# A fused vision tower: moving attention's product with V behind the next scores, and the FFN weights' quantising forward

## The chip, the cores and the metric

One core of one Trainium2 chip. The time is the device time of one execution in microseconds. The kernel before takes 271.56 us, the median of 3 runs (271.5 to 272.1).

## The reference

A two-layer tower on 16 images of 36 tokens (T = 576) and 192 channels: patch embedding, attention with 12 heads of 64, a feed-forward layer (FFN) with quantised weights and activations, then a second layer (test-time-training attention and 8 experts) that the change does not touch. Cut to the part concerned:

```
h = patches @ W_proj.T + b_proj
xn = layernorm(layernorm(h)) * gamma + beta
q, k, v = split(xn @ w_qkv)                       # 12 heads of 64
out = softmax(q @ k.T / 8) @ v                    # within an image: 36 keys
h = h + out @ w_out + b_out

def weight_quant(w):                              # FFN weights w_in, w_out
    scale = 1.0 / max(mean(abs(w)), 1e-5)
    return clip(round(w * scale), -1, 1) / scale
h = h + bitlinear(gated(bitlinear(layernorm(h), w_in)), w_out)
... second layer
```

## The kernel before

Every engine has one hand-written instruction stream; engines meet through semaphores. In a stream, an instruction that waits holds up everything behind it.

**Precision.** Nearly every fp32 operand x is split into two f16 parts, a high one (ACT copies x to f16) and a low one (DVE forms x minus the high part). A product is three f16 products, so most results leave PSUM twice: first by ACT (high), then by DVE (low), which also frees the bank.

**PSUM.** The 8 banks go round in the order of `plan(...)`, which is the order of PE's work. PE claims a bank when its last user has been read (`claim`); `wait_full` waits for a bank to be filled, `wait_evac` for it to be read, `frees` marks that.

**Order of the stages.** Embedding, normalisation, V for five tiles of 128 tokens (L552), two pairs of small products for the sums of the FFN weights' magnitudes (L558, L559), keys and queries for the first 8 images (L568), then the attention loop with `PAIRS + 4` = 12 turns s = 0 to 11, then the rest of the output projection and the FFN.

**The attention loop** is a software pipeline over pairs of images, PAIRS = 8. In turn s:

- PE: the product with V of pair s-4 (L609, `values`), the transposes of the probabilities of pair s-3, high and low part into two banks (L623), in turns 0 to 2 four banks of keys and queries of the second 8 images (`keys_queries`, L568), the scores of pair s+1 (L597, `scores`), in turns 8 to 10 a tile of the output projection (L582).
- DVE: the sum of the exponentials of pair s-1 (L1064) and its reciprocal (L1067), the maximum of the scores of pair s (L1071) and the subtraction (L1074), the low half of the probabilities of pair s-2 (L1081), in turns 0 to 2 the low halves of two heads' keys (L1018) and queries (L1025), the low half of the product with V of pair s-4 (L1090), and the work laid between: the clipping of the FFN weights, w_out (`stage2`, L1093, L1094) in turn 3 and w_in (`stage13`, a view of `stage_a`, L1096, L1098) in turns 4 and 5; the low half of the attention's w_out (L1101) in turn 7, which the output projection awaits (`wo_lo`); preparation of layer 2's weights (`state_weights`) in turn 9; residuals (L1054) from turn 9.
- GpSimd (POOL): the probabilities times the reciprocals (L1797).
- ACT: the high half of the probabilities of pair s-2 (L1545), the high half of the product with V of pair s-4 (L1549), the copy of the transposed high part of pair s-3 (L1556), exp of pair s (L1559), the copy of the transposed low part (L1563), in turns 0 to 2 high halves of keys and queries (L1529, L1534), the attention's w_out to f16 (L1569) in turn 5, the quantised FFN w_out (L1575) in turn 6; behind the loop the quantised w_in (L1577) and a table load.

The means of the FFN weights are finished on DVE (L1007 to L1012) before the first keys are read. The raw attention w_out (`woraw`) is loaded by SP behind the 32 loads of V; it lies in the arena that GpSimd's expert weights use later, so these wait for `wo_lo` (`expert_high`).

Of the kernel before, what the change touches and what calls it, by code (L numbers as in the profile page):

```python
# [23 lines left out]
FH = 512  # L24
# [20 lines left out]
NROW = _at  # L45

# [5 lines left out]
def tower(nc, d, out):  # L52

    ctx = ExitStack()
    with ctx:
# [241 lines left out]
        plan("wmean")  # L297
# [4 lines left out]
        for s in range(PAIRS + 4):  # L302
            if 0 <= s - 4:
                plan("PV", s - 4)
# [3 lines left out]
            if s < 3:  # L308
                for hp in (2 * s, 2 * s + 1):
                    plan("k", hp, 1)  # L310
                    plan("q", hp, 1)
            if s + 1 < PAIRS:
                plan("S", s + 1)
            if PAIRS <= s < PAIRS + 3:
                plan("wo", s - PAIRS)
# [107 lines left out]
        def expert_high(pool, e):  # L423
# [3 lines left out]
            if e == 4:  # L427
                wait_full(pool, "S", PAIRS - 1)
                pool.wait_ge(wo_lo, 1)
# [21 lines left out]
        def _(sp):  # L451
# [34 lines left out]
            wait_full(sp, "q", HP - 1, 1)  # L486
# [27 lines left out]
        def _(pe):  # L514
# [40 lines left out]
            bk = claim(pe, "wmean")  # L555
            pe.wait_ge(wq_part, 2)
            pe.wait_ge(zeroed, 1)
            mm(bk[:, 0:1], ones[0:HF, :].broadcast_to([HF, 128]), wsum[0:HF, 0:1], start=True, stop=True)  # L558
            ins = mm(bk[:, 1:2], ones[:, :].broadcast_to([128, 128]), wsum[:, 1:2], start=True, stop=True)  # L559
            fills(ins, "wmean")  # L560
# [53 lines left out]
            for s in range(PAIRS + 4):  # L614
                if 0 <= s - 4:
                    values(s - 4)
# [8 lines left out]
                if s < 3:  # L625
                    for hp in (2 * s, 2 * s + 1):
                        keys_queries(hp, 1)
                if s + 1 < PAIRS:
                    scores(s + 1)
                if PAIRS <= s < PAIRS + 3:  # L630
# [311 lines left out]
        def _(dve):  # L942
# [48 lines left out]
            dve.wait_ge(loaded("w_in"), 16)  # L991
            dve.wait_ge(loaded("w_out2"), 16)
            v.tensor_reduce(wsum[0:HF, 0:1], stage13[:, :, :], AX.XY, ALU.add, apply_absolute_value=True).then_inc(wq_part, 1)
            v.tensor_reduce(wsum[:, 1:2], stage2[:, :, :], AX.XY, ALU.add, apply_absolute_value=True).then_inc(wq_part, 1)
# [9 lines left out]


            bk = wait_full(dve, "wmean")
            st_.do(v.tensor_scalar(mw[:, 0:1], bk[:, 0:1], 1.0 / (2 * FH * D), 1e-5, ALU.mult, ALU.max))  # L1007
# [949 lines left out]
```

## Time and profile before

| | us |
|---|---|
| median of 3 runs | 271.56 |
| the profiled execution | 269.44 |
| its span, first to last instruction | 267.6 |
| PE busy in the span | 223.1 |
| DVE busy | 191.0 |
| ACT busy | 154.6 |
| GpSimd busy | 115.9 |

The busy times are averages over stages with different limits. The attention loop runs from about 51 to 102 us. The rows further below come from its timeline: each line gives start, length, engine, source line, operation, output and inputs with their shapes, the number of instructions merged, and in brackets how long the engine had been idle and what it waited for ("issue" where the profile shows no releaser). Instructions on DVE and ACT overlap a little: the next starts up to 0.1 us before the end of the last.

### The profile page before, as it was taken

What the parts mean: (1) busy time and instruction counts of PE and PEld (TensorE: products, weight loads), DVE (VectorE), ACT (ScalarE), POOL (GpSimd) and SP (SyncE); (2) the same over time, 40 slices, a digit from 0 to 9 for tenths busy, and PEclk for the clock granted to TensorE, in tenths of its full rate; (3) what the DMA queues carried; (4) which work ended last, traced back from release to release, by engine and by line L of the source; (5) the groups of instructions that cost most, each with busy time, mean ns of one, the idle gap of its engine ahead of it and who ended that gap; (6) DMA issues with size and microseconds to landing.
All of it is one profiled execution on the core that took longest, in us unless ns stands there. A gap on an engine that the chain in (4) does not pass through costs nothing.

```text
span 267.6 us, 6168 instructions
## 1 busy us (share of the span) xinstructions
PE 223.1 (83%) x2338; PEld 174.5 (65%) x2338; DVE 191.0 (71%) x520; ACT 154.6 (58%) x296; POOL 115.9 (43%) x139
## 2 busy tenths in 40 slices
PE   1964999797396897797989999899899695999992
PEld 1741467586396896344458596786648595899982
DVE  1749979767999577869958869649786352655575
ACT  4639467355679755378579758557461265455610
POOL 9112495011122696476390002502602887867710
PEclk9996599999779599999999999999999999999997
DMA  6999352332540049993009001994290599883362
GB/s 213 336 257 216 82 224 65 71 69 68 164 146 4 2 67 205 212 210 67 4 0 108 2 0 10 119 138 62 13 173 12 100 147 160 144 124 31 35 154 66
DMA packets 24786, 28.66 MB, mean 107 GB/s; under 512 B 11544, under 2 KB 19793, under 8 KB 24533
## 3 DMA queue, kind: packets, MB, share of 16 engines
q0 software_dynamic: 6624, 13.66, 34.0%
q1 hardware_dynamic: 18133, 14.60, 19.2%
q8 instruction: 19, 0.31, 0.5%
q14 instruction: 10, 0.08, 0.1%
HBM read 34.98 MB, written 4.81 MB: 149 GB/s over the span
## 4 chain that ended last, share of the span: by engine, by line
PE 43%; DVE 26%; ACT 9%; issue 8%; POOL 1%; DMA 1%; another core or an unknown queue 1%; DVEq 0%; ACTq 0%; POOLq 0%
PE bank L885 7%; PE bank L896 5%; PE bank L552 5%; PE bank L637 4%; PE bank L568 3%; PE bank L727 2%; PE bank L609 2%; DVE arena_k L1018 2%; PE bank L597 2%; PE bank L704 2%; PE bank L582 2%; DVE st L949 2%; PE bank L834 1%; DMA arena<-x_scratch,arena 1%; PE bank L745 1%
## 5 line engine op out<-in xcount | busy, mean ns | idle before, releaser
L637 PE MATMUL bank<-tri,idh 128*128 128x512 f16 x148 | 38.5, 380 | 0.0
L1797 POOL TENSOR_TENSOR arena<-arena,ri 128x432 f32<-128x432 f32 x8 | 7.5, 942 | 39.3 <-DVE ri L1067 39.3
L1773 POOL TENSOR_TENSOR rs<-arg,mhalf 128x1 f32<-128x1 f32 (+1 forms) x20 | 11.9, 596 | 23.1 <-DVE arg L953 21.6
L1875 POOL DMA_INDIRECT arena<-x_scratch,arena x14 | 14.1, 1006 | 16.7 <-DVE arena L1431 12.7
L1866 POOL DMA_INDIRECT y_sum<-arena x12 | 18.2, 1515 | 6.3 <-issue 2.9
L1383 DVE TENSOR_TENSOR arena<-bank,arena 128x360 f32<-128x360 f32 x16 | 8.4, 532 | 16.8 <-PE bank L885 8.5
L637 PEld LDWEIGHTS bank<-tri,idh 128*128 128x128 f16 x148 | 13.7, 98 | 9.7
L568 PE MATMUL bank<-arena,arena_k 96*128 96x288 f16 (+2 forms) x144 | 18.3, 286 | 0.0
L525 PE MATMUL bank<-arena_v,arena 128*128 128x192 f16 (+1 forms) x90 | 11.6, 295 | 5.9 <-DVE arena_v L967 5.9
L568 PEld LDWEIGHTS bank<-arena,arena_k 96*128 96x128 f16 x144 | 13.8, 98 | 3.5
L885 PE MATMUL bank<-arena,arena_v 128*128 128x180 f16 x160 | 13.4, 240 | 2.9 <-DVE arena L1372 2.6
L597 PE MATMUL bank<-arena_k,arena 128*64 128x72 f16 x288 | 11.3, 210 | 5.0 <-DVE arena L1025 5.0
L444 POOL DMA_DIRECT2D arena_v<-in_w x4 | 3.2, 806 | 27.2 <-ACT arena_v L439 27.2
L885 PEld LDWEIGHTS bank<-arena,arena_v 128*128 128x128 f16 x160 | 12.4, 97 | 4.0 <-DVE arena L1372 3.3
L597 PEld LDWEIGHTS bank<-arena_k,arena 128*64 128x64 f16 x288 | 10.4, 122 | 6.4 <-issue 6.3
L552 PE MATMUL bank<-arena_k,arena 96*128 96x384 f16 (+1 forms) x60 | 13.3, 394 | 1.5 <-DVE arena_k L980 1.5
L525 PEld LDWEIGHTS bank<-arena_v,arena 128*128 128x128 f16 (+1 forms) x90 | 9.0, 119 | 8.3 <-DVE arena_v L967 6.2
L1018 DVE TENSOR_TENSOR arena_k<-bank,arena_k 64x288 f16<-64x288 f32 x24 | 10.9, 454 | 4.5 <-ACT arena_k L1529 3.9
L1784 POOL MEMSET arena_v<- 72x12288 f32 x1 | 10.3, 10338 | 7.0 <-DVE arena_k L990 7.0
L1724 ACT ACTIVATE arena<-bank 128x360 f32<-128x360 f32 x16 | 7.3, 470 | 10.5 <-PE bank L885 9.4
L885 PE MATMUL bank<-arena,arena_k 128*128 128x180 f16 x160 | 13.1, 240 | 0.0
L609 PE MATMUL bank<-arena,arena_v 72*128 72x36 f16 x288 | 9.0, 183 | 4.5 <-issue 4.5
(286 smaller groups left out, 634.2 us busy)
## 6 DMA issues: line engine op xcount, KB each, us to landing
arena_k<-in_w POOLq DMA_DIRECT2D x8, 512.0 KB, 6.4
arena_v<-in_w POOLq DMA_DIRECT2D x8, 512.0 KB, 10.2
arena_v<-in_xT SPq DMA_DIRECT2D x6, 288.0 KB, 3.7
arena_v<-in_wqkv SPq DMA_DIRECT2D x3, 576.0 KB, 10.0
arena_v<-v_scratch SPq DMA_DIRECT2D x32, 54.0 KB
v_scratch<-arena SPq DMA_DIRECT2D x4, 384.0 KB, 2.6
arena_k<-in_w POOLq DMA_DIRECT2D x8, 192.0 KB, 7.2
arena_v<-in_w POOLq DMA_DIRECT2D x8, 192.0 KB, 11.2
```

The source lines that it names most:

```text
L525: ins = mm(at_bank("embed", i)[0:r, 0:D], xpT[:, a_, k, 128 * i:128 * i + r], wp16[:, w_, k, :], start=k == 0 and n == 0, stop=k == KC - 1 ...
L552: ins = mm(bk[0:r, 0:384], x16[:, a_, j, 128 * i:128 * i + r], wqkv[:, w_, j, 1536 + 384 * c:1536 + 384 * c + 384], start=n + j == 0, stop ...
L568: ins = mm(bk[:, 0:c1 - c0], wqkv[:, w_, j, o + 128 * hp:o + 128 * hp + 128], x16[:, a_, j, c0:c1], start=m + j == 0, stop=m == 2 and j == 1)
L597: ins = mm(bk[64 * x:64 * x + 64, 72 * hp:72 * hp + 72], qT[:, a_, hp, NP * b:NP * b + 64], Kbd[:, w_, hp, b, :], start=n == 0, stop=n == 2)
L609: ins = mm(bk[:, 72 * hp + NP * x:72 * hp + NP * x + NP], Vbd[:, 2 * p + x, hp].rearrange("p y c x -> p (y c) x")[:, :, w_], PT[:, p % 2, ...
L637: mm(bank[IDLE][:, :], idh[:, :], tri[:, 0:1].broadcast_to([128, 512]), start=True, stop=True)
L885: ins = mm(bk[:, CAP * m:CAP * m + CAP], w[:, wx, j, f:f + 128], z[:, zx, :], start=n == 0, stop=n == 4)
L896: ins = mm(bk[0:SH, D * s:D * s + D], actp2[e % 2][:, ax, m, SH * s:SH * s + SH], w2p[e][:, wx, m, :], start=n == 0, stop=n == 11)
L1018: ins = v.tensor_tensor(Kbd[o, 1, hp, 8 * n:8 * n + 8, NP * x:NP * x + NP], bk[o, 0:288].rearrange("p (b k) -> p b k", k=NP), Kbd[o, 0, hp ...
L1773: g.tensor_tensor(rs[0:r, o + i:o + i + 1], arg[0:r, o + i:o + i + 1], half_[0:r, 0:1], ALU.pow).then_inc(sem_out, 1)
L1866: nc.gpsimd.indirect_dma_start(y_sum[k][:, :], bass.IndirectOffsetOnAxis(ap=sum_at[:, k, e:e + 1], axis=0), ys[:, e, D * k:D * k + D], Non ...
L1875: nc.gpsimd.indirect_dma_start(zr[:, e - 1, XW * k:XW * k + XW], None, x_scr[:, :], bass.IndirectOffsetOnAxis(ap=tok_at[:, k, e:e + 1], ax ...
```

## The change

On PE the product with V moves to the end of its turn, behind the transposes and the next scores. Its two read-outs move as well: on ACT behind exp and the copy of the low transposed part, and on both engines a turn later for the first pairs (pair s-5 in turns 5 to 7, pairs 3 and 4 in turn 8, then pair s-4). The sums of the FFN weights' magnitudes are taken by ACT (Abs with an accumulated sum) between the first keys and the loop, not by DVE before V is read; the products that spread them move from in front of the keys into turn 0, and the means into DVE's turn 0. The clipping moves from turns 3 to 5 to turns 1 and 2, the quantising copies from turn 6 and from behind the loop to turns 2 and 3. `woraw` lies in another arena, and two waits go (SP's before its load, GpSimd's for `wo_lo`).

```diff
+def read_out(s):
+    if s < PAIRS:
+        return range(max(s - 5, 0), max(s - 4, 0))
+    return range(PAIRS - 5 if s == PAIRS else s - 4, s - 3)
...
+        wide = arena[:, KC * T + HP * D:KC * T + HP * D + 2048]
-        woraw = arenaK[:, K_W:K_W + HP * D].rearrange("p (k n) -> p k n", k=HP)
+        woraw = arena[:, KC * T:KC * T + HP * D].rearrange("p (k n) -> p k n", k=HP)
...
-                pool.wait_ge(wo_lo, 1)
...
-            wait_full(sp, "q", HP - 1, 1)
...   # PE; the order of plan() follows it
-            bk = claim(pe, "wmean")   # and its four products
+            def weight_sums():        # the same
             scores(0)
             for s in range(PAIRS + 4):
-                if 0 <= s - 4:
-                    values(s - 4)
                 p = s - 3             # transposes
                 if s < 3:
-                    for hp in (2 * s, 2 * s + 1):
-                        keys_queries(hp, 1)
+                    keys_queries(2 * s, 1)
+                    if s == 0:
+                        weight_sums()
+                    keys_queries(2 * s + 1, 1)
                 if s + 1 < PAIRS:
                     scores(s + 1)
+                if 0 <= s - 4:
+                    values(s - 4)
...   # DVE
-            v.tensor_reduce(wsum[0:HF, 0:1], stage13[:, :, :], AX.XY, ALU.add, apply_absolute_value=True).then_inc(wq_part, 1)
-            v.tensor_reduce(wsum[:, 1:2], stage2[:, :, :], AX.XY, ALU.add, apply_absolute_value=True).then_inc(wq_part, 1)
...   # in the loop, behind the low half of the probabilities
+                if s == 1:
+                    st_.then(v.tensor_scalar(stage2[:], stage2[:], sw[:, 1:2], 1.0, ALU.mult, ALU.min))
+                    v.tensor_scalar(stage2[:], stage2[:], -1.0, MAGIC, ALU.max, ALU.add).then_inc(wq_sum, 1)
+                if s == 2:
+                    st_.settle()
+                    v.tensor_scalar(stage13[:], stage13[:], -1.0, MAGIC, ALU.max, ALU.add).then_inc(wq_sum, 1)
                 if s < 3:
-                    for hp in (2 * s, 2 * s + 1):
-                        kq_low(hp, 1)
-                p = s - 4
-                if 0 <= p:
+                    kq_low(2 * s, 1)
+                if s == 0:
+                    weight_means()
+                if s == 1:
+                    st_.do(v.tensor_scalar(stage13[:], stage13[:], sw[0:HF, 0:1], 1.0, ALU.mult, ALU.min))
+                if s < 3:
+                    kq_low(2 * s + 1, 1)
+                for p in read_out(s):
                     bk = wait_full(dve, "PV", p)
                     dve.wait_ge(ao_hi, p + 1)   # and the subtraction into aoT
-                if s == 3: ...  if s == 4: ...  if s == 5: ...   # the same four passes
...   # ACT, before the loop
+            act.wait_ge(loaded("w_in"), 16)
+            act.wait_ge(loaded("w_out2"), 16)
+            act.wait_ge(v_stored, 16 * NT)
+            for w, n in ((stage_a[0:HF, :], 0), (stage2[:, :, :].rearrange("p m n -> p (m n)"), 1)):
+                r, m = w.shape
+                st_.do(a(wide[0:r, 0:m], w, ACT.Abs, accum_out=wsum[0:r, n:n + 1]))
+                st_.settle()
+            act.sem_inc(wq_part, 2)
...   # ACT, in the loop: behind the high half of the probabilities
-                p = s - 4
-                if 0 <= p:
-                    bk = wait_full(act, "PV", p)
-                    a(aoT[:, 0, :, 72 * p:72 * p + 72], ...).then_inc(ao_hi, 1)
...   # behind exp and the copy of the low transposed part
+                for p in read_out(s):
+                    bk = wait_full(act, "PV", p)
+                    a(aoT[:, 0, :, 72 * p:72 * p + 72], ...).then_inc(ao_hi, 1)
                 if s < 3: ...                   # high halves of keys and queries
+                if s == 2:
+                    act.wait_ge(wq_sum, 1)
+                    a(w2q[:], stage2[:], ACT.Identity, bias=nmagic[:, 0:1]).then_inc(wq_done, 1)
+                if s == 3:
+                    act.wait_ge(wq_sum, 2)
+                    a(wiq[:], stage13[:], ACT.Identity, bias=nmagic[0:HF, 0:1]).then_inc(wq_done, 1)
-                if s == 6: ...                  # w2q
-            act.wait_ge(wq_sum, 2)              # wiq, behind the loop
```

## Rows read from the trace of the kernel before

**Rows 1.** The page, granted clock: tenths of full speed, 40 equal slices.
```profile
PEclk9996599999779599999999999999999999999997
```

**Rows 2.** Timeline, DVE: start, length, engine, line, tiles, count [idle <-releaser].
```profile
60.85 0.92 DVE L1018 TENSOR_TENSOR arena_k<-bank,arena_k 64x288 f16<-64x288 f32 x2 [1.41 <-ACT arena_k L1529]
...
66.81 0.92 DVE L1018 TENSOR_TENSOR arena_k<-bank,arena_k 64x288 f16<-64x288 f32 x2 [0.90 <-ACT arena_k L1529]
```

**Rows 3.** Timeline, DVE, turns 3 to 7: sums (L1064), clipping, scores.
```profile
69.40 0.59 DVE L1064 TENSOR_REDUCE sm<-arena 128x12 f32<-128x432 f32 x1
...
72.92 0.60 DVE L1064 TENSOR_REDUCE sm<-arena 128x12 f32<-128x432 f32 x1
...
75.23 2.01 PE L597 MATMUL bank<-arena_k,arena 128*64 128x72 f16 x36
...
75.83 1.27 DVE L1096 TENSOR_SCALAR stage_a<-stage_a,sw 96x2048 f32<-96x2048 f32 x1
...
77.14 0.60 DVE L1064 TENSOR_REDUCE sm<-arena 128x12 f32<-128x432 f32 x1
...
81.19 0.59 DVE L1064 TENSOR_REDUCE sm<-arena 128x12 f32<-128x432 f32 x1
...
84.09 0.59 DVE L1064 TENSOR_REDUCE sm<-arena 128x12 f32<-128x432 f32 x1
...
88.27 0.59 DVE L1064 TENSOR_REDUCE sm<-arena 128x12 f32<-128x432 f32 x1
```

**Rows 4.** Timeline, turns 5 to 7: ACT and DVE.
```profile
82.46 0.81 ACT L1556 ACTIVATE arena<-bank 72x768 f16<-72x768 f16 x1
...
82.54 0.61 DVE L1074 TENSOR_TENSOR arena<-bank,mx 128x432 f32<-128x432 f32 x1
...
83.18 0.56 ACT L1559 ACTIVATE arena<-arena 128x432 f32<-128x432 f32 x1
...
83.65 0.79 ACT L1563 ACTIVATE arena<-bank 72x768 f16<-72x768 f16 x1
...
84.34 0.92 ACT L1575 ACTIVATE w2q<-stage,nmagic 128x768 f16<-128x768 f32 x1
...
87.00 1.34 DVE L1101 TENSOR_TENSOR arena<-arena_k,arena 128x1152 f16<-128x1152 f32 x1
```

**Rows 5.** Timeline, tail of the attention stage: PE, ACT, DVE.
```profile
88.10 1.24 PE L609 MATMUL bank<-arena,arena_v 72*128 72x36 f16 x36 [1.82 <-issue]
...
90.44 3.09 PE L582 MATMUL bank<-arena 128*128 128x192 f16 x18
...
94.37 0.84 PE L623 MATMUL bank<-idh,arena 128*72 128x128 f16 x12
...
94.56 0.53 ACT L1549 ACTIVATE arena<-bank 128x432 f16<-128x432 f32 x1 [1.76 <-PE bank L609]
...
95.05 1.65 PE L582 MATMUL bank<-arena 128*128 128x192 f16 x18
...
95.19 0.61 DVE L1090 TENSOR_TENSOR arena<-bank,arena 128x432 f16<-128x432 f32 x1 [1.19 <-ACT arena L1549]
```

**Rows 6.** Timeline, before the first scores: means of the weights, ACT's wait.
```profile
39.16 0.38 PE L558 MATMUL bank<-wsum,ones 96*128 96x1 f32 x2
...
40.46 0.13 DVE L1007 TENSOR_SCALAR mw<-bank 128x1 f32<-128x1 f32 x1
...
40.84 0.56 DVE L1012 TENSOR_SCALAR mwd<-mw 128x2 f32<-128x2 f32 x1
...
53.51 0.56 ACT L1559 ACTIVATE arena<-arena 128x432 f32<-128x432 f32 x1 [3.96 <-DVE arena L1074]
```

**Rows 7.** Timeline, ACT behind the attention loop.
```profile
101.49 1.99 ACT L1577 ACTIVATE wiq<-stage_a,nmagic 96x2048 f16<-96x2048 f32 x1
...
103.49 1.28 ACT L1497 ACT_TABLE_LOAD   x1
...
108.56 0.47 ACT L1584 ACTIVATE arena<-bank,nmagic 96x256 f16<-96x256 f32 x1 [3.57 <-PE bank L648]
```

More of the change, by code:

```diff
@@ L311, in tower @@
                     plan("q", hp, 1)
+                    if hp == 0:
+                        plan("wmean")
             if s + 1 < PAIRS:
                 plan("S", s + 1)
+            if 0 <= s - 4:
+                plan("PV", s - 4)
             if PAIRS <= s < PAIRS + 3:
@@ L554, in _ @@
                     fills(ins, "v", i, c)
-            bk = claim(pe, "wmean")
[L556 to L560, printed above, removed]
+            def weight_sums():
+                bk = claim(pe, "wmean")
+                pe.wait_ge(wq_part, 2)
+                pe.wait_ge(zeroed, 1)
+                mm(bk[:, 0:1], ones[0:HF, :].broadcast_to([HF, 128]), wsum[0:HF, 0:1], start=True, stop=True)
+                ins = mm(bk[:, 1:2], ones[:, :].broadcast_to([128, 128]), wsum[:, 1:2], start=True, stop=True)
+                fills(ins, "wmean")
             def keys_queries(hp, n):
@@ L1058, in _, with weight_means @@
             dve.wait_ge(hbias, 1)
+            def weight_means():
+                bk = wait_full(dve, "wmean")
+                st_.do(v.tensor_scalar(mw[:, 0:1], bk[:, 0:1], 1.0 / (2 * FH * D), 1e-5, ALU.mult, ALU.max))
+                frees(v.tensor_scalar(mw[:, 1:2], bk[:, 1:2], 1.0 / (FH * D), 1e-5, ALU.mult, ALU.max), "wmean")
+                st_.settle()
+                wait_evac(dve, "wmean")
+                st_.do(v.reciprocal(sw[:], mw[:]))
+                st_.then(v.tensor_scalar(mwd[:], mw[:], 1.0 / 127.0, None, ALU.mult))
             for s in range(PAIRS + 4):
@@ L1091, in _ @@
                                           ALU.subtract), "PV", p)
-                if s == 3:
-                    st_.then(v.tensor_scalar(stage2[:], stage2[:], sw[:, 1:2], 1.0, ALU.mult, ALU.min))
-                    v.tensor_scalar(stage2[:], stage2[:], -1.0, MAGIC, ALU.max, ALU.add).then_inc(wq_sum, 1)
-                if s == 4:
-                    st_.then(v.tensor_scalar(stage13[:], stage13[:], sw[0:HF, 0:1], 1.0, ALU.mult, ALU.min))
-                if s == 5:
-                    v.tensor_scalar(stage13[:], stage13[:], -1.0, MAGIC, ALU.max, ALU.add).then_inc(wq_sum, 1)
                 if s == PAIRS - 1:
@@ L1563, in _ @@
                     frees(a(PT[:, p % 2, 1, :], bk[0:72, :].bitcast(F16)[:, 0:768], ACT.Copy), "PT", p, 1)
+                for p in read_out(s):
+                    bk = wait_full(act, "PV", p)
+                    a(aoT[:, 0, :, 72 * p:72 * p + 72], bk[:, 0:432].rearrange("p (h q) -> p h q", h=HP),
+                      ACT.Copy).then_inc(ao_hi, 1)
                 if s < 3:
@@ L1572, in _ @@
                     a(wa16[:, 0], wa[:, :, :], ACT.Copy).then_inc(tw_hi, 1)
-                if s == 6:
-                    act.wait_ge(wq_sum, 1)
-                    a(w2q[:], stage2[:], ACT.Identity, bias=nmagic[:, 0:1]).then_inc(wq_done, 1)
-            act.wait_ge(wq_sum, 2)
-            a(wiq[:], stage13[:], ACT.Identity, bias=nmagic[0:HF, 0:1]).then_inc(wq_done, 1)
             table(ACT.Silu)
```

16 lines of the change are left out of this document (2 added, 14 removed).

## The prediction, made before the result

> **What bounds the kernel now.** Start with the granted clock on the page, one digit for each 6.7 us [rows 1]. In the attention stage (50 to 102 us) the digits 7, 7 (67 to 80 us) and 5 (87 to 94 us) say that TensorE falls to its lower level (1.2 GHz) there twice, so PE is not what is full: the stage is a chain over four engines, and the question is which wait closes its turn. The timeline answers that. A turn runs from one start of L1064 (DVE's sum of the exponentials) to the next.
>
> - Turns 0 to 2, 5.96 us each, are DVE's: maximum, subtraction, then a hole while ACT does exp and the first copy of keys (1.41 us in turn 1, 0.90 us in turn 2 [rows 2]), then the low halves of keys and queries without a gap.
> - Turns 3, 4 and 5 take 72.92 - 69.40 = 3.52, 77.14 - 72.92 = 4.22 and 81.19 - 77.14 = 4.05 us [rows 3]. DVE has no hole in them: the clipping of the FFN weights lies there (L1096 takes 1.27 us).
> - Turn 6 has no clipping and takes 2.90 us (81.19 to 84.09), turn 7 has woT's low half (L1101, 1.34 us) and takes 4.18 us [rows 3, 4].
> - After that PE leads. The product with V at 88.10 had waited 1.82 us, and the first output projection, at the slow clock, takes 3.09 us where a later one takes 1.65 us [rows 5].
>
> The end hangs on DVE's in-order queue. L1090 of pair 5 starts at 95.19 [rows 5]. Behind it come the state weights and residual(0), whose bank output projection 2 needs, then PV(7), its two read-outs, residual(2) and the FFN. The change touches nothing in that row of work, so I carry one number through: the start of L1090 for pair 5.
>
> **The change part by part.** Everything is counted in the profiled execution (269.44 us, span 267.6 us). The runs of before have the median 271.56 us, 2.12 us above it; I add my difference to the median.
>
> *Sums of the weights off DVE, onto ACT.* DVE loses two reductions before 34 us. They bring nothing: the keys start by PE's order, behind V, and DVE waits for ACT's first copy of keys, not ACT for DVE. PE loses the small products between V and K. The first pair takes 0.38 us and all of K waits behind it [rows 6], so **-0.38 us**; at most twice that, and 0 if DVE's read-out of V decides there. ACT's two Abs passes come where ACT waits 3.96 us for the first scores [rows 6]. By L1577, 2048 columns in 1.99 us [rows 7], 2048 and 768 columns cost 1.99 + 0.75 us; that leaves 1.22 us of the hole for reading out the two sums and the two settles, of which no row shows the cost. The hole opens and closes with the keys and moves as a whole; I take **0**, and each us beyond 1.22 would be a us of the stage.
>
> *Means on DVE, moved to turn 0* between two low halves. From L1007's start at 40.46 to L1012's end at 41.40 it is 0.94 us [rows 6]. It used to lie before the first keys were there; now it lies behind turn 0's hole, where DVE has no other, so **+0.94 us** (0 to 0.94).
>
> *Clipping moved.* stage2's two passes (turn 1) fall into the hole of 1.41 us and cost nothing. stage13's first pass stands between the low halves of turn 1, behind the hole: **+1.27 us**. Its second pass (turn 2, taken as 1.27 us like the first, same tile) meets a hole of 0.90 us: **+0.37 us**. Turn 2 thus ends 2.20 us later. The lower bound for all of this is 0, if ACT's copies rather than DVE set these turns.
>
> *Turn 3* loses its clipping and has no read-out. DVE then waits for exp: L1074 starts 1.35 us into a turn, exp starts 0.64 us later and takes 0.56 us, plus 0.05 us [rows 3, 4]: 2.60 instead of 3.52 us, **-0.92 us**.
>
> *Turn 4.* The quantising of w_in (L1577, 1.99 us [rows 7]) moves from behind the loop, where ACT later sat idle for 3.57 us waiting for PE [rows 7] (so nothing is gained there), to ACT's turn 3. Behind it in ACT's queue are the high half of P(2), the copy of PT(1) and exp(4); DVE's next sum waits for that. Start to start on ACT [rows 4, 5, 7]: from exp(3) 0.47 to the copy of PT(0), 0.69 to w_in, 1.90 to the high half of P(2) (1.99 less an overlap of 0.09), 0.45 from that (as many columns as the 0.53 us read-out, less the overlap) to the copy of PT(1), 0.72 (0.81 less the same) to exp(4). That is 4.23 us from exp to exp, and the sums behind them stand as far apart: **0** against turn 4's 4.22. w2q (0.92 us) moves into turn 2, where ACT waits for DVE's subtraction anyway: 0.
>
> *Turns 5 to 7: the read-out.* This is the step that I think decides. ACT's high half of PV used to stand before exp in ACT's turn, so that it was done when DVE came to L1090. Now it stands behind exp and behind the copy of PT's low part, while DVE's L1090 still stands before DVE's next sums, and the next exp waits for DVE's subtraction. That closes a loop in every turn. From L1074's start: exp +0.64, copy +0.47, read-out on ACT +0.69 (the next start behind the copy), its 0.53 us, +0.10 to L1090, +0.51 to the sum (0.61 less the overlap), +1.35 to the next L1074 (81.19 to 82.54) [rows 4, 5]: **4.29 us**. DVE stands idle for about 1.2 of it. Turn 5 was 4.05 (**+0.24**), turn 6 was 2.90 (**+1.39**), and turn 7, with L1101's 1.27 us (87.00 to 88.27), comes to 5.56 instead of 4.18 (**+1.38**). Bounds: 2.90 us a turn if DVE never waits for that read-out, and 4.7 us a turn if PE runs at the lower clock (1.24 for PV, 2.01 for the scores, twice the quick 0.84 for the transposes [rows 3, 5], less some 0.2 of overlap).
>
> Sum up to the sum of pair 7: -0.38 + 0.94 + 1.27 + 0.37 - 0.92 + 0 + 0.24 + 1.39 + 1.38 = **+4.29 us**, so 92.56 instead of 88.27.
>
> *The tail gives part back.* PE's new order no longer holds the transposes behind the product with V, so PT(5) and PV(4) are done while woT's low half is awaited. The first output projection starts 0.1 us after 92.56. Then it takes 1.65 us quick or 3.09 us slow [rows 5]; PE has worked for some 2 us before it, so I take the middle, 2.4. Then PT(6) 0.84, PV(5) 1.24, +0.05, ACT's 0.53, +0.10: L1090 for pair 5 at 92.56 + 5.26 = 97.82, against 95.19. The tail costs 5.26 instead of 6.92 us: **-1.66 us** (-0.97 to -2.41 by the two clocks). Turn 8 reads out pairs 3 and 4 together, which ACT and DVE have done before PV(5) is ready.
>
> *The rest* costs nothing: woT lands in another place but is issued at the same point of SP's queue, after the loads of V; GpSimd's wait for wo_lo goes, but behind its last product with the reciprocals it has rows of its own to make first, and the weight's low half behind those waits for ACT's turn 8. From residual(0) on everything moves as a whole.
>
> Result: +4.29 - 1.66 = **+2.63 us**: 272.1 us in a profile like this one, and as a median **274.2 us**.
>
> **Two rules beside the rows.** Of the clock, the rows show that the digit falls to 5 around the product that had waited 1.82 us [rows 1, 5]. The Trainium skill, page "TensorE: Matmul & The Clock Gate", section "Why this matters for your kernels", says that idle gaps between bursts of products send the clock back to its lower level. A loop in which PE waits for DVE in every turn leaves such gaps. By that rule the first output projection would be slow throughout, and the sum +3.3 us; by the middle of the two rows it is the +2.63 above. Of tables, the row shows that one load takes 1.28 us [rows 7]. The skill's page "ScalarE: Activation LUTs", section "Table sets: the hidden batching unit", says that abs is in every set; by that the Abs passes bring no load, and by the opposite the third rival below holds.
>
> **The rivals.**
> 1. *Faster: the loop through the read-out doesn't bind.* PE's waits for ACT's copies go (1.82 us once [rows 5]), and turns 5 to 7 run at DVE's 2.90 us. That takes (4.29 - 2.90) x 3 = 4.17 us off: 2.63 - 4.17 = -1.54 us, **270.0 us**. For it: PE's order is better by itself. Against: the order on ACT and DVE, as above. It decides once DVE's wait before L1090 is under 0.6 us a turn.
> 2. *PE becomes the bound at the slow clock.* Turns 5 to 7 take 4.7 us (+1.2) and the first output projection 3.09 us (+0.7): +4.5, **276.1 us**. It decides from the point where PE's three pieces of a turn pass 4.29 us. For it: the clock digits after a pause. Against: the digit is 9 from 80 to 87 us [rows 1], through turn 6.
> 3. *The Abs passes reload tables.* Two loads of 1.28 us [rows 7] on top of 2.74 us, and half of the 1.22 us for the reads, overrun the 3.96 us by 1.95: 2.63 + 1.95, **276.1 us**.
> 4. *No difference.* The three insertions of turns 0 to 2 fall into slack, because ACT's copies set those turns (-2.58 us, so +0.05): **271.6 us**. Against: DVE goes from one low half to the next without a gap.
>
> **How the numbers follow.** My forecast 0.50 (its own range 273.4 to 275.2), rival 1 0.13, rival 2 0.20, rival 3 0.05, rival 4 0.12. A change under 0.2% (0.54 us) can't be told from none here. Faster is rival 1, 0.13; the same is rival 4, 0.12; slower is the rest, 0.75. The range 271.0 to 276.2 leaves out rival 1 and the upper edge of rivals 2 and 3, under 2 in 10.
>
> **What would show it.** In the profile after: the first L568 product some 0.4 us earlier; no table load between 40 and 60 us; the hole before turn 1's low halves filled, that turn near 7.2 us; turn 3 near 2.6 us; in turns 5 to 7 DVE idle for some 1.2 us each before the low read-out of PV, released by ACT's high one, with 4.3 us from sum to sum; the first output projection released by woT's low half near 92.6 us; the low read-out of pair 5 near 98 us; all after that unchanged in length. The forecast is wrong if that idle time is missing, or if the stretch from the first scores to the last low read-out is not longer than before.

## The result and the profile after

Over 4 runs the changed kernel takes 275.79 us (274.44 to 277.68) beside 271.83 us before: 1.0144 times as long, 95% interval 1.0092 to 1.0195, or +3.9 us (the 271.83 is the three runs of before given above and one more). Timed again among the experiments (12 runs beside 29 of before) it stands at 1.0088 (1.0050 to 1.0125), +2.4 us. All ratios here leave out the executions that took over 1.5% longer than the fastest of the same kernel. The change makes the kernel slower: neither interval reaches 1. In the two profiled executions the last read-out of attention (DVE, pair 7) starts at 104.88 us instead of 101.69: +3.19 us.

The page after, its span and the granted clock:

```profile
span 272.6 us, 6168 instructions
...
PEclk9996699998588589999999999999999999999996
```

From 61 to 102 us, the turns and the tail, the clock's digits are 8, 5, 8, 8, 5, 8; before, the low ones were 7, 7 and 5 [rows 1]. The tail's fall to the lower clock (the second 5, 89 to 95 us) is still there.

The timeline of the changed kernel, DVE's sums of the exponentials (L1069, L1064 before), the starts of turns 3 to 8:

```profile
70.66 0.59 DVE L1069 TENSOR_REDUCE sm<-arena 128x12 f32<-128x432 f32 x1
...
73.25 0.60 DVE L1069 TENSOR_REDUCE sm<-arena 128x12 f32<-128x432 f32 x1
...
77.44 0.60 DVE L1069 TENSOR_REDUCE sm<-arena 128x12 f32<-128x432 f32 x1 [0.47 <-ACT arena L1570]
...
81.75 0.59 DVE L1069 TENSOR_REDUCE sm<-arena 128x12 f32<-128x432 f32 x1
...
86.05 0.59 DVE L1069 TENSOR_REDUCE sm<-arena 128x12 f32<-128x432 f32 x1
...
91.61 0.60 DVE L1069 TENSOR_REDUCE sm<-arena 128x12 f32<-128x432 f32 x1
```

Read as differences, turns 3 to 7 take 2.59, 4.19, 4.31, 4.30 and 5.56 us. Before they took 3.52, 4.22, 4.05, 2.90 and 4.18 [rows 3]. So turn 3 gained, turn 4 is as long as before for another reason, and turns 5 to 7 lost 3.04 us together.

Why they lost it stands in turn 6 of the same timeline (DVE's subtraction, ACT's exp, its copy of the low transposed part, its high read-out, DVE's low read-out):

```profile
83.10 0.61 DVE L1079 TENSOR_TENSOR arena<-bank,mx 128x432 f32<-128x432 f32 x1
...
83.74 0.56 ACT L1570 ACTIVATE arena<-arena 128x432 f32<-128x432 f32 x1 [0.42 <-DVE arena L1079]
...
84.21 0.79 ACT L1574 ACTIVATE arena<-bank 72x768 f16<-72x768 f16 x1
...
84.90 0.52 ACT L1577 ACTIVATE arena<-bank 128x432 f16<-128x432 f32 x1
...
85.52 0.61 DVE L1105 TENSOR_TENSOR arena<-bank,arena 128x432 f16<-128x432 f32 x1 [1.29 <-ACT arena L1577]
```

Each line starts within 0.1 us of the end of the one above, and in front of the last one DVE was idle for 1.29 us. The waits of the changed kernel from 74 to 106 us, summed (total us, how many, the longest), have this as DVE's largest:

```profile
DVE arena L1105 <- ACT arena L1577: 7.5, 5, 2.7
```

Before the changed part, the same timeline shows ACT's sums and DVE's means:

```profile
48.77 1.90 ACT L1552 ACTIVATE arena<-stage_a 96x2048 f32<-96x2048 f32 x1
...
51.55 0.19 ACT L1552 ACTIVATION_READ_ACCUMULATOR arena<-stage 128x1 f32 x1
...
52.83 0.56 ACT L1570 ACTIVATE arena<-arena 128x432 f32<-128x432 f32 x1 [1.10 <-DVE arena L1079]
...
55.51 0.15 DVE L1058 TENSOR_SCALAR mw<-bank 128x1 f32<-128x1 f32 x1
...
56.09 0.92 DVE L1014 TENSOR_TENSOR arena_k<-bank,arena_k 64x288 f16<-64x288 f32 x2
```

ACT's two passes with their reads end at 51.74, and exp still waited 1.10 us for DVE: the passes are covered [rows 6: 3.96]. There is no table load among them. The means now hold the next low half up by 0.58 us, not 0.94.

The tail (PE's transposes after a wait, its first output projection, its transposes, the low read-out of pair 5, a GpSimd and a DVE instruction, output projection 2, the last low read-out):

```profile
88.67 0.82 PE L628 MATMUL bank<-idh,arena 128*72 128x128 f16 x6 [1.96 <-DVE arena L1086]
...
91.75 3.06 PE L589 MATMUL bank<-arena 128*128 128x192 f16 x18 [1.11 <-DVE arena L1109]
...
94.61 1.49 PE L628 MATMUL bank<-idh,arena 128*72 128x128 f16 x12
...
97.84 0.61 DVE L1105 TENSOR_TENSOR arena<-bank,arena 128x432 f16<-128x432 f32 x1 [2.67 <-ACT arena L1577]
...
97.98 1.65 POOL L1793 TENSOR_TENSOR arena_k<-wa,arena_k 96x768 f16<-96x768 f32 x1 [0.18 <-POOL rows L1821]
...
98.83 0.83 DVE L1034 TENSOR_SCALAR b1m<-b1m 108x12 f32<-108x12 f32 x1
...
101.67 1.65 PE L589 MATMUL bank<-arena 128*128 128x192 f16 x18 [1.40 <-DVE h L1050]
...
104.88 0.61 DVE L1105 TENSOR_TENSOR arena<-bank,arena 128x432 f16<-128x432 f32 x1 [0.96 <-ACT arena L1577]
```

The first output projection is slow (3.06 us), so are the transposes (1.49 instead of 0.84 us [rows 5]). The granted clock is 0.50 all the way from 87 to 97 us. Behind pair 5's read-out a scalar operation on 108x12 elements takes 0.83 us on DVE and ends when GpSimd's L1793 ends; output projection 2 then waits 1.40 us for the residual.

The end of the execution, from the chain that ended last in the changed kernel:

```profile
236.36 6.79 DMA y_sum<-arena
```

Here the adding of the experts' rows into memory ended last (before, the chain ran through PE's products of the experts instead), and the shift, 3.2 us at 205 us, grew to 5.0 us. I do not count that growth as the change's: from the FFN's first transposes to the end the profiled executions of all these kernels take 158.7 to 163.5 us, and the one of before, with 159.6, is near the lower end.

One place that varies can be named. These are the first product with w_in in the FFN of this profile and in that of the same kernel, unedited, timed again (e8):

```profile
114.12 1.89 PE L667 MATMUL bank<-wiq,arena 96*128 96x512 f16 x8
```

```profile
113.67 3.47 PE L667 MATMUL bank<-wiq,arena 96*128 96x512 f16 x8
```

PE's waits just before are the same in both (0.54 and 1.35 us), but in e8 the granted clock is 0.50 from 114 to 116 us and here it is 1.00. Counted from the sum of pair 0, the layer-2 products behind it (L680) start at 62.13 us here and at 63.79 in e8; before it was 58.86. So two executions of one kernel can lie 1.7 us apart there by that clock alone. It need not reach the end: from the first transposes on, e8 takes 161.2 us and this profile 161.4.

### The profile page after: what moved, and what is told of

It is laid out like the page before. It is cut to its first block, busy times and chain, and to the rows that moved or that the text cites. A ratio compares the mean times of both kernels' runs of the same rounds, so it can differ in the third digit from the quotient of the medians.

```text
span 272.6 us, 6168 instructions
## 1 busy us (share of the span) xinstructions
PE 224.4 (82%) x2338; PEld 175.5 (64%) x2338; DVE 188.6 (69%) x518; ACT 157.2 (58%) x300; POOL 117.0 (43%) x139
## 3 DMA queue, kind: packets, MB, share of 16 engines
q1 hardware_dynamic: 18133, 14.60, 19.1%
## 4 chain that ended last, share of the span: by engine, by line
DVE 29%; PE 25%; issue 11%; POOL 10%; DMA 8%; ACT 7%; DVEq 0%; SPq 0%; POOLq 0%; ACTq 0%
DMA y_sum<-arena 6%; PE bank L558 5%; POOL arena L1891 4%; PE bank L646 4%; PE bank L575 3%; POOL y_sum L1882 3%; PE bank L736 2%; DVE arena_k L1014 2%; PE bank L713 2%; PE bank L589 2%; DMA arena_v<-y_sum 2%; DVE st L958 2%; DVE arena L1079 2%; DVE mx L1076 1%; DVE sm L1069 1%
## 5 line engine op out<-in xcount | busy, mean ns | idle before, releaser
L1891 POOL DMA_INDIRECT arena<-x_scratch,arena x14 | 14.9, 1061 | 16.7 <-DVE arena L1439 12.7
L628 PE MATMUL bank<-idh,arena 128*72 128x128 f16 x96 | 9.2, 255 | 5.2 <-DVE arena L1086 5.0
L894 PEld LDWEIGHTS bank<-arena,arena_k 128*128 128x128 f16 x160 | 12.5, 97 | 1.5 <-DVE arena L1380 1.5
```

Source lines behind the costliest of these rows:

```text
L628: ins = tr(bk[0:72, :].bitcast(F16)[:, 128 * hp:128 * hp + 128], P16[:, p % 2, c, 72 * hp:72 * hp + 72], idh[:])
L894: ins = mm(bk[:, CAP * m:CAP * m + CAP], w[:, wx, j, f:f + 128], z[:, zx, :], start=n == 0, stop=n == 4)
L1891: nc.gpsimd.indirect_dma_start(zr[:, e - 1, XW * k:XW * k + XW], None, x_scr[:, :], bass.IndirectOffsetOnAxis(ap=tok_at[:, k, e:e + 1], ax ...
```

## The experiments

All are compared with the kernel before, run beside them on the same chip. Lengths in the table are from each kernel's profile: turns 4 to 7, then from the sum of pair 0 to the sum of pair 7, and from there on to the last low read-out.

| kernel | ratio to before (95%) | turns 4, 5, 6, 7 | to sum 7 | on to the last read-out |
|---|---|---|---|---|
| before | 1 | 4.22, 4.05, 2.90, 4.18 | 30.79 | 13.42 |
| changed | 1.0144 (1.0092 to 1.0195) | 4.19, 4.31, 4.30, 5.56 | 34.22 | 13.27 |
| e8, changed again | 1.0088 (1.0050 to 1.0125) | 4.19, 4.30, 4.29, 5.56 | 34.20 | 13.27 |
| e1, read-out before exp | 0.9983 (0.9940 to 1.0027) | 4.19, 2.92, 3.56, 4.19 | 30.72 | 14.39 |
| e2, before with late read-out | 1.0282 (1.0233 to 1.0331) | 6.09, 5.44, 4.29, 5.56 | 36.81 | 13.30 |
| e4, attention part only | 1.0146 (1.0089 to 1.0203) | 3.70, 5.44, 4.29, 5.56 | 34.43 | 13.25 |
| e5, weights' part only | 1.0019 (0.9983 to 1.0055) | 4.61, 3.91, 3.76, 4.28 | 32.42 | 13.26 |
| e3, residual first | 0.9997 (0.9960 to 1.0035) | 4.18, 4.31, 4.30, 5.55 | 34.20 | 11.59 |
| e9, PE kept busy | 1.0155 (1.0097 to 1.0214) | 4.19, 4.31, 4.29, 5.56 | 34.21 | 14.60 |
| e10, e1 with GpSimd clear | 1.0054 (1.0012 to 1.0095) | 4.19, 2.92, 3.56, 4.19 | 30.70 | 12.54 |
| e6, e1 and residual first | 0.9920 (0.9882 to 0.9957) | 4.19, 2.91, 3.56, 4.19 | 30.72 | 11.06 |
| e7, e6 and two orders more | 0.9892 (0.9845 to 0.9939) | 2.60, 3.46, 3.76, 4.19 | 29.87 | 11.03 |
| e11, before with two orders | 1.0017 (0.9971 to 1.0063) | 4.23, 4.05, 2.91, 4.29 | 30.92 | 12.32 |
| e12, e11 and attention well ordered | 0.9980 (0.9924 to 1.0036) | 3.70, 4.05, 2.91, 4.17 | 30.27 | 12.60 |

**e1: the read-out in front of exp.** My theory was the loop; rivals were PE's order and the weights' moves.

```diff
                     a(P16[:, p % 2, 0, :], P[:, p % 3, :], ACT.Copy).then_inc(p_hi, 1)
+                for p in read_out(s):          # the high read-out, four lines
...
-                for p in read_out(s):          # no longer behind the copy of the low part
```

> The changed kernel with one thing undone: ACT reads out the product with V (high half) right behind the high half of the probabilities, in front of the copy of the transposed high part and of exp, as before; the turn in which a pair is read out stays the changed one. Theory (the loop exp, copy, high read-out, low read-out, sums, subtraction closes turns 5 to 7): turns 5, 6 and 7, 4.31, 4.30 and 5.56 us in the changed kernel, fall to about 3.1, 3.1 and 4.4 (PE's three pieces then bound them), DVE no longer waits before its low read-out, and the time falls by 2.5 to 3.5 us, to about the time of the kernel before or a little under it. Rival A (the new order on PE itself is what costs): turns 5 to 7 stay near 4.3 and the time near 1.014 of before. Rival B (the weight work in turns 0 to 2 is what costs): the time falls by under 1 us.

Measured: 0.9983. The four sums that start turns 5 to 8, then the tail (low read-out of pair 5, GpSimd's L1793, a DVE instruction, output projection 2):

```profile
76.61 0.60 DVE L1069 TENSOR_REDUCE sm<-arena 128x12 f32<-128x432 f32 x1 [0.47 <-ACT arena L1574]
...
79.53 0.59 DVE L1069 TENSOR_REDUCE sm<-arena 128x12 f32<-128x432 f32 x1
...
83.09 0.60 DVE L1069 TENSOR_REDUCE sm<-arena 128x12 f32<-128x432 f32 x1 [0.37 <-ACT arena L1574]
...
87.28 0.59 DVE L1069 TENSOR_REDUCE sm<-arena 128x12 f32<-128x432 f32 x1
...
91.73 0.59 DVE L1105 TENSOR_TENSOR arena<-bank,arena 128x432 f16<-128x432 f32 x1
...
93.54 1.73 POOL L1793 TENSOR_TENSOR arena_k<-wa,arena_k 96x768 f16<-96x768 f32 x1 [0.18 <-POOL rows L1821]
...
93.70 1.62 DVE L1038 TENSOR_TENSOR w1s<-w1s,wmean 96x32 f32<-96x32 f32 x1
...
96.88 3.04 PE L589 MATMUL bank<-arena 128*128 128x192 f16 x18 [3.03 <-DVE h L1050]
```

Turns 5 to 7 fall from 4.31, 4.30, 5.56 to 2.92, 3.56, 4.19 us, the loop is gone, and what the change cost no longer shows. But the low read-out of pair 5, which comes 2.5 us earlier than before counted from the sum of pair 0 (3.5 on the clock of the profiles), gains nothing at the end: the last read-out is 0.9 us later than before by the same count. DVE's L1038, 96x32 elements, takes 1.62 us (0.18 before) beside GpSimd's L1793, the residual comes late, PE waits 3.03 us and works on at the lower clock (3.04 instead of 1.65 us).

**e2: the kernel before with the late read-out alone.**

```diff
-                p = s - 4                      # the high read-out of pair s-4, in front of the copies and exp
...
                     frees(a(PT[:, p % 2, 1, :], bk[0:72, :].bitcast(F16)[:, 0:768], ACT.Copy), "PT", p, 1)
+                p = s - 4                      # the same, behind the copy of the low part
```

> The kernel before with one thing done: ACT reads out the product with V behind exp and behind the copy of the transposed low part, same pair in the same turn, PE and everything else as before. Theory: the same loop closes, 4.29 us without the work that DVE has behind its read-out in a turn, so turn 6 goes from 2.90 to 4.3, turns 4, 5 and 7 (with 1.27 us each behind the read-out) from 4.22, 4.05 and 4.18 to about 5.5: +5.5 us at the sum of pair 7, of which the tail gives back up to 1.5: +4 to +5.5 us, 1.015 to 1.020 of before. Rival A (PE's order is what costs): within 0.5 us of before.

Measured: 1.0282. Sums of turns 4 to 8, and in turn 6 the low read-out:

```profile
72.38 0.60 DVE L1064 TENSOR_REDUCE sm<-arena 128x12 f32<-128x432 f32 x1
...
78.47 0.60 DVE L1064 TENSOR_REDUCE sm<-arena 128x12 f32<-128x432 f32 x1
...
83.91 0.59 DVE L1064 TENSOR_REDUCE sm<-arena 128x12 f32<-128x432 f32 x1
...
87.67 0.61 DVE L1090 TENSOR_TENSOR arena<-bank,arena 128x432 f16<-128x432 f32 x1 [1.29 <-ACT arena L1562]
...
88.20 0.59 DVE L1064 TENSOR_REDUCE sm<-arena 128x12 f32<-128x432 f32 x1
...
93.76 0.60 DVE L1064 TENSOR_REDUCE sm<-arena 128x12 f32<-128x432 f32 x1
```

Turn 6 is 4.29 us with nothing of the change but ACT's order, as worked out; turns 5 and 7 are 5.44 and 5.56. Turn 4 came to 6.09, over my 5.5 (there ACT's first copy also waited 1.59 us for transposes that took 1.48 us), and the time rose by 7.6 us where I had said 4 to 5.5: I had let the tail give something back, and from sum 7 on it is no shorter (13.30 against 13.42 us). The last read-out is 5.9 us later than before, counted from the sum of pair 0; in the FFN's front the first product with w_in also ran at the lower clock in this profile (3.27 us), and the layer-2 products start 7.6 us later than before.

**e4 and e5: the two parts of the change apart.** e4 is the kernel before with PE's order and both read-outs of the change; e5 is the changed kernel with these three undone.

```diff
+def read_out(s): ...
-                if 0 <= s - 4:                 # PE: values(s - 4) behind scores(s + 1)
-                    values(s - 4)
...
                 if s + 1 < PAIRS:
                     scores(s + 1)
+                if 0 <= s - 4:
+                    values(s - 4)
```

> The kernel before with the attention part of the change alone: PE's order (transposes, next scores, product with V), the later read-outs on ACT and DVE; the weights' sums, means, clipping and quantising stay where they were. Theory: turns 5 and 7 have 4.3 us of loop plus the 1.27 us of work behind the read-out (clipping in turn 5, woT's low half in turn 7), turn 6 has 4.3, turns 3 and 4 have no read-out and stay at 3.5 and 3.9: +3.5 to +4.5 us at the sum of pair 7, 1.0 to 2.5 given back in the tail: +2 to +3.5 us. If the weight part is what costs, it is at or under before.

Measured: 1.0146, as much as the whole change and above the 2 to 3.5 us that I had said; turn 6 is 4.29 us.

> The kernel before with the weights' part alone: sums on ACT, their spreading products and the means in turn 0, clipping in turns 1 and 2, quantising in turns 2 and 3, woT in the other arena; PE's order and the read-outs as before. Theory: turns 0 to 2 end about 1.2 us later, as measured in the changed kernel (70.66 against 69.40), turns 3 to 5 lose their clipping (1.1, 1.3 and 1.1 us) but turn 4 waits for ACT's quantising of w_in; turns 4 to 7 then close on the loop of PE's product with V behind ACT's copy of the low part, about 3.5 us; together -0.5 to -2 us at the sum of pair 7, so 269.8 to 271.5 us. Rival B (these moves are what costs): +1 us or more over before.

Measured: 1.0019 (0.9983 to 1.0055). I had expected a gain of 0.5 to 2 us; there is none. The clipping that left turns 3 to 5 came back in turns 1 and 2, turn 4 (4.61 us) has DVE waiting for ACT behind the quantising of w_in, and turn 6 rose to 3.76: the sum of pair 7 is 1.6 us later than before, where I had said 0.5 to 2 us earlier. In time that doesn't show beyond the interval.

**e3: the residual in front of the preparation of weights.**

```diff
-                if s == PAIRS + 1:
-                    state_weights()
                 if s >= PAIRS + 1:
                     residual(s - PAIRS - 1)
+                if s == PAIRS + 1:
+                    state_weights()
```

> The changed kernel with one order turned round on DVE in turn 9: the residual of tile 0 in front of the preparation of layer 2's weights, not behind it. In the changed kernel output projection 2 waited 1.40 us for that residual (its bank), and the preparation had grown to 2.80 us. Theory (the tail behind pair 5's read-out is set by DVE's order there, not by PE): the first product of output projection 2 starts right behind the product with V of pair 6, about 100.3 instead of 101.7, and the time falls by about 1.4 us. Rival (PE's own work sets the tail): within 0.5 us of the changed kernel, 1.013 to 1.015 of before.

Measured: 0.9997. The last read-out is 1.68 us nearer to sum 7, as expected (1.4), so the tail is set by DVE's order there. The ratios say more, 2.5 to 4 us by the two ratios of the changed kernel; their intervals are 1 to 1.4 us either way, and no trace shows the rest. Against before, the last read-out is still 1.6 us later, counted from the sum of pair 0, though the ratio shows no difference. So the ratios are too coarse to place a microsecond, and the loop, which is untouched here, is shown by the turns.

**e9: PE kept busy through its waits.**

```diff
+            def junk(bk, n):
+                for _ in range(n):
+                    mm(bk[:, :], idh[:, :], idh[:, 0:1].broadcast_to([128, 512]), start=True, stop=True)
             def output_projection(i):
+                if i == 0:
+                    junk(claim(pe, "wo", 0), 5)
                 pe.wait_ge(wo_lo, 1)
...
+                        if (p, c) == (5, 1):   # between the two transposes of pair 5
+                            junk(bk, 8)
```

> The changed kernel with 13 idle products of 512 columns on PE where it waits: 8 between the two transposes of pair 5, 5 in front of the first output projection (its result is overwritten, the output is the same). Tests the clock's share in the tail. If the lower clock is what made it 6.23 us from the sum of pair 7 to pair 5's low read-out instead of the 5.26 I took: the granted clock stays full from 84 to 100 us, the first output projection takes 1.65 instead of 3.06 us, transposes 0.84 instead of 1.49, pair 5's low read-out comes 1.5 to 2.3 us earlier, and the time falls by 1.0 to 2.3 us. If the tail isn't PE's: no difference in time though the products are faster.

Measured: 1.0155, no gain. The windows from 88 to 96 us (length, busy time of PE, PE's loads, DVE, ACT and GpSimd with counts, granted clock, DMA's share and GB/s), first the changed kernel, then e9:

```profile
88.00:92.00 4.00, 2.22 (x44) 2.02 (x45) 2.70 (x5) 3.96 (x8) 0.00 (x0) 0.50 0.02 6
...
92.00:96.00 4.00, 4.00 (x33) 3.86 (x32) 2.71 (x6) 2.15 (x4) 3.45 (x4) 0.50 0.00 0
```

```profile
88.00:92.00 4.00, 4.00 (x64) 3.02 (x63) 3.53 (x7) 3.74 (x7) 0.84 (x1) 0.96 0.01 4
...
92.00:96.00 4.00, 4.00 (x84) 4.00 (x82) 2.33 (x7) 2.48 (x4) 3.92 (x7) 1.00 0.00 0
```

The clock is up and the low read-out of pair 5 comes 4.78 instead of 6.23 us behind sum 7: 1.45 us by the clock. It is lost at once:

```profile
96.84 1.63 DVE L1046 TENSOR_TENSOR w1s<-w1s,wmean 96x32 f32<-96x32 f32 x1
...
100.03 3.04 PE L595 MATMUL bank<-arena 128*128 128x192 f16 x18 [2.87 <-DVE h L1058]
```

DVE's small instruction is held for 1.63 us again, PE waits 2.87 us for the residual and falls to the lower clock itself. The quicker PE only waits longer: in the changed kernel it waited 1.40 us there, stayed at the full clock and took 1.65 us.

**e10: GpSimd's instruction elsewhere.** On e1:

```diff
-            weight_low(0, wa, wa16)            # L1793
             for e in (4, 5, 6):
                 expert_high(pool, e)
             for i in range(3):
                 power(ln_arg, NT + i + 1, i, 0, ln_pow)
+            weight_low(0, wa, wa16)
```

> The kernel with the high read-out in front of exp (0.998 of before), and one GpSimd instruction elsewhere: the low half of wa, 1.73 us, which stood at the time of DVE's preparation of layer 2's weights, goes behind the powers of tiles 0 to 2. DVE's order stays. In that kernel the preparation took 4.13 us from its first start to the residual of tile 0, and its longest instruction (96x32, 1.62 us instead of 0.18) ended 0.05 us behind GpSimd's. Theory (DVE is held by GpSimd's access until that ends): the preparation falls to 2.3 to 2.8 us, output projection 2 starts 1.3 to 1.8 us earlier and PE's wait in front of it falls from 3.03 to about 1.4 us, so the time falls by about 1 to 2 us, to 0.991 to 0.995. Rival (the preparation is slow for another reason, semaphores or its own chain): it stays near 4 us.

Measured: 1.0054 (1.0012 to 1.0095). The same DVE instruction, output projection 2, where GpSimd's went, and PE in the front of the FFN:

```profile
93.73 0.18 DVE L1038 TENSOR_TENSOR w1s<-w1s,wmean 96x32 f32<-96x32 f32 x1
...
95.45 2.64 PE L589 MATMUL bank<-arena 128*128 128x192 f16 x18 [1.58 <-DVE h L1050]
...
102.22 1.63 POOL L1793 TENSOR_TENSOR arena_k<-wa,arena_k 96x768 f16<-96x768 f32 x1
...
102.26 1.80 DVE L1122 SCALAR_TENSOR_TENSOR xc<-h,mv,rows 128x192 f32<-128x192 f32 x1
...
107.57 0.42 PE L657 MATMUL bank<-idf,xc 128*96 128x128 f32 x2 [1.93 <-DVE h L1050]
...
111.32 2.72 PE L667 MATMUL bank<-wiq,arena 96*128 96x512 f16 x8
```

The place is as expected: L1038 takes 0.18 us, the preparation 2.68 instead of 4.13, projection 2 starts 1.4 us earlier and PE waits 1.58 us. The time is not: I had said 0.991 to 0.995. The instruction now meets DVE in the front of the FFN, where L1122 takes 1.80 instead of 0.42 us. Even so the FFN's first transposes (L657) come 1.6 us earlier than in e1, counted from the sum of pair 0. What comes next takes that back and more: PE waits 1.93 us in front of them and 1.34 us behind them, the granted clock is 0.50 from 110 to 113 us (1.00 in e1), and the first product with w_in takes 2.72 us instead of 1.89. The layer-2 products behind it (L680) start at 60.95 us from the sum of pair 0, in e1 at 59.76. So there e10 is 1.2 us behind e1, where the ratios are 1.9 us apart. This is a hint and not more: from there to the end this profile takes 152.9 us and that of e1 155.3, and e8 has the fall of the clock too, with no edit at all. Why the whole time is longer stays open.

**e6 and e7: both orders, then two more.** e6 is e1 with e3's edit. e7 adds:

```diff
+            for i in range(3):                 # GpSimd: powers in front of the loads
+                power(ln_arg, NT + i + 1, i, 0, ln_pow)
             for e in (4, 5, 6):
                 expert_high(pool, e)
-            for i in range(3):
-                power(ln_arg, NT + i + 1, i, 0, ln_pow)
...
-                if s == 3:                     # ACT: wiq, back behind the loop
```

> The changed kernel with both orders turned: ACT's high read-out of the product with V in front of exp, and the residual of tile 0 in front of the preparation of layer 2's weights. With the first alone, pair 5's low read-out came at 91.7 (before: 95.2) but the residual only at 96.4, since the preparation took 4.1 us beside GpSimd's work, and PE waited 3.03 us and fell to the lower clock. Theory (the gain of the early read-out was lost to that residual): output projection 2 starts near 93.9 and pair 7's low read-out near 97.5 instead of 101.7; GpSimd's powers, behind its expert loads, then bound the FFN's start, so 2 to 4 us under before: 0.985 to 0.993. Rival (the early read-out's gain was lost to the clock, whatever the order): within 1 us of the early read-out alone, 0.998.

> As the last one, and GpSimd makes the powers of tiles 0 to 2 in front of its loads of experts 4 to 6, and ACT quantises w_in behind the loop as in the kernel before. Theory: turn 4, 4.19 us in the changed kernel because ACT's 1.99 us stand in front of exp(4), falls to about 3 us, and the powers are no bound: another 0.5 to 1.5 us under the last one, 0.980 to 0.990. If turn 4 was not ACT's, it stays at 4.2.

Measured: e6 0.9920, e7 0.9892. The sums that start turns 4, 5 and 8 and output projection 2 in e7:

```profile
72.10 0.60 DVE L1069 TENSOR_REDUCE sm<-arena 128x12 f32<-128x432 f32 x1
...
74.70 0.60 DVE L1069 TENSOR_REDUCE sm<-arena 128x12 f32<-128x432 f32 x1
...
86.11 0.60 DVE L1069 TENSOR_REDUCE sm<-arena 128x12 f32<-128x432 f32 x1
...
92.52 1.65 PE L589 MATMUL bank<-arena 128*128 128x192 f16 x18
```

Turn 4 fell from 4.19 to 2.60 us: it had been ACT's quantising of w_in. Projection 2 has no wait in front of it and runs at full clock. e7 takes 268.85 us beside 272.04, the fastest version. Its interval and e6's overlap, so what the two last orders bring in time isn't shown. By the traces e7 is 0.9 us ahead of e6 at the FFN's first transposes, but 0.6 us behind it at the layer-2 products (57.07 against 56.43 us from the sum of pair 0), since PE then waits 1.32 us for DVE.

**e8, e11 and e12: controls.** e8 is the changed kernel unedited. e11 is the kernel before with e3's edit and e7's powers. e12 is e11 with PE's new order and e1's read-out, but none of the weights' part.

> The changed kernel, nothing edited, beside the next two on one chip. So far it stands at 1.0144 of before (1.0092 to 1.0195, 4 runs), while turning one order on DVE brought it to 0.9997, which is more than the 1.7 us that the trace of that run shows. If the 1.0144 holds, the median is 3.3 to 4.3 us above before; if it was high by chance, it comes to 1.005 to 1.010, which fits the +3.2 us of the traces at the end of attention less the start's scatter.

> The kernel before with the two orders that helped the changed one: the residual of tile 0 in front of the preparation of layer 2's weights, and GpSimd's powers in front of its loads of experts 4 to 6. In the kernel before output projection 2 waited only 0.16 us for that residual. Theory (before, PE's chain behind ACT's copies sets the tail, so these orders have nothing to free): 0 to 0.7 us under before, 0.997 to 1.000. Rival (the gain of 0.989 is from these orders alone, and the change's parts bring nothing): 0.989 to 0.993.

> The kernel before with PE's new order, the high read-out on ACT in front of exp, a turn later for the first pairs, and the two orders of the last one; the weights' sums, means, clipping and quantising stay as in the kernel before. Tells what the weights' part is worth in a kernel whose loop doesn't close. Turns 0 to 2 are 5.96, 5.96 and 3.52 us instead of 7.16, 6.11 and 2.59, and turns 4 and 5 carry 1.3 and 1.2 us of clipping (about 4.0 us each instead of 2.6 and 3.5): the sum of pair 7 within 0.5 us of that of the kernel with both (86.1), so 0.987 to 0.993 if the weights' part is worth nothing, 0.994 or more if it is worth over 1 us.

Measured: e8 1.0088; e11 1.0017 (0.9971 to 1.0063), so those orders alone bring the kernel before nothing that shows in time (its tail is 1.1 us shorter), and e7's gain isn't theirs alone; e12 0.9980 (0.9924 to 1.0036), with 5 of its 12 executions from 269.4 to 272.5 us and 7 from 273.7 to 275.5, too wide to say what the weights' part is worth (the ratio goes by the 5). By the traces e7 reaches the sum of pair 7 in 29.87 us and e12 in 30.27: 0.4 us.

## Why the prediction was right

It forecast +2.63 us and 274.2 us; measured are +3.9 and, again, +2.4 us. The 275.79 us lies in the range of 271.0 to 276.2 but above the 273.4 to 275.2 that the forecast had given itself. Point by point, by its own steps:

- **The sums, the means and PE's products.** Over these and the clipping I had +2.20 us at the start of turn 3; measured 70.66 - 69.40 = +1.26. The means were 0.58 instead of 0.94, and K started 0.67 us earlier instead of 0.38. The second is not clean: the first copy of keys starts at 38.6 to 40.6 us in the profiled executions.
- **Clipping.** Turn 1 was to be near 7.23 and is 7.16 us; turn 2 was to be 6.33 and is 6.11.
- **Turns 3 and 4.** 2.60 and 4.23 worked out, 2.59 and 4.19 measured. That turn 4 is ACT's quantising is shown by e7.
- **Turns 5 to 7, the step that decides.** 4.29, 4.29 and 5.56 worked out; 4.31, 4.30 and 5.56 measured. e1 takes the loop out of the changed kernel, e2 puts it alone into the kernel before; both move the turns as they should, and the time the right way (e2 by more than worked out).
- **The tail.** Here a size was off: I took the middle of the two clocks for the first output projection (2.4 us), and it ran at the lower one, with the transposes behind it (3.06 and 1.49): 6.23 instead of 5.26 us. From start to start that is 0.46 us for the projection and 0.44 for the transposes. The granted clock fell between 86.5 and 87 us, at the start of the 1.96 us wait that ends at 88.67; PE had stood idle for 0.64 and 0.23 us in the turn before it, and the clock stayed down until 97 us. The rule of the Trainium skill that I had set beside it (page "TensorE: Matmul & The Clock Gate", section "Why this matters for your kernels": idle gaps between bursts send the clock down) pointed the right way.
- **"From residual(0) on everything moves as a whole"** failed by 0.54 us: 7.04 instead of 6.50 us between the last two read-outs I had carried. The row shows DVE's 108x12 operation at 0.83 instead of 0.17 us, held until GpSimd's L1793 ended; in e10, with GpSimd's instruction elsewhere, the operation held in the same place in e1 takes 0.18 us. The Trainium skill, page "SBUF — State Buffer", section "Who interferes with whom", says that DVE and GpSimd share a pair of ports, which the instruction that comes first keeps to its end; these traces agree (1.62, 1.63 and 0.83 us, in e1, e9 and the changed kernel, each over within 0.05 us of GpSimd's end).

Two errors cancelled: the sum of pair 7 came 0.95 us earlier than worked out (91.61 for 92.56), the tail took 0.97 us longer, and so the low read-out of pair 5, worked out for 97.82, came at 97.84. That this number fits is luck; the turns, which the account rests on, are right one by one. Of the 3.9 us first measured, 3.2 stand at the end of attention; no trace shows the rest to be the change's.

Rival 1 (PE's order is better by itself) was false for the change; with the read-out in front of exp, turn 5 does run at 2.92 us (e1), and e6 and e7 are faster than before. How much of that is PE's order isn't settled, since e12 is too wide. Rival 2 (PE at the slow clock) came half true: the first output projection took 3.06 us, but turns 5 and 6 took 4.3 us and not 4.7. Rival 3 is false, as no table load lies there. Rival 4 (the insertions fall into slack) holds for a part: 0.94 of the 2.20 us up to the start of turn 3 didn't come.

## What to carry to other kernels

Before moving a step behind others on one engine, write down who reads its result and what that engine does next: if the reader stands in front of the work that the first engine waits for, the two queues close a loop in every turn, and its length is a plain sum of rows. A gain upstream is worth what the next in-order queue lets through: here one residual, behind a preparation that grew from 2.26 to 4.13 us in e1, swallowed all of it. And count a gain by its own edits taken back one at a time: with one step of it put back this change costs nothing that shows (0.9983), and with the residual in front as well it gains (0.9920).

## What the runs showed of the hardware

Small DVE instructions that work on SBUF alone (not on PSUM) were held until a GpSimd instruction ended. In nine of the fourteen profiled executions one of two in the preparation (96x32 or 108x12 elements, 0.17 to 0.18 us when free) took 0.73 to 1.63 us and ended 0.03 to 0.05 us behind GpSimd's L1793; in the other five L1793 was over, or within 0.1 us of its end, when they started. A 128x192 one went from 0.42 to 1.80 us and ended 0.21 us behind it (e10). Not every instruction is held: in the changed kernel, beside the same L1793, DVE's reductions (L1032, L1033) took 0.34 and 0.17 us and the low read-out, with one operand in PSUM, 0.61 us, as they did before.

PE's lower clock went where the waits went, but not with every wait: the granted clock is 1.00 from 89 to 98 us in e9 and 0.50 from 99 on, in the wait of 2.87 us; the changed kernel's wait of 1.40 us at 101 us left it at 1.00. I had not expected how little a faster PE is worth while its waits only move, nor that one and the same kernel can have the first product with w_in at either level (1.89 and 3.47 us).
